# Centring a mixing matrix on TensorE, taking a variance by squares on ScalarE, and building the expert tables once

## The reference, cut to what matters

```
x = x + layernorm(attn(layernorm(x)))      # first half
x = x + layernorm(moe(layernorm(x)))       # second half

attn(y): Q, K, V = y Wq' + bq, y Wk' + bk, y Wv' + bv
         Q, K scaled to unit norm over the tokens
         tailor = 1 / (256 + Q . (sum K + 1e-6));  matrix = K' V
         return y + gamma * (sum V + Q matrix) * tailor
moe(y):  the two best of 8 experts for each token, e(y) = gelu(y W1 + b1) W2 + b2, plus a shared layer
layernorm(z) = (z - mean z) / sqrt(var z + 1e-5)
```

## Time and profile before

| | |
|---|---|
| time before, median of 3 runs | 691.05 us (690.42 to 691.43) |
| the profiled execution's own time | 688.41 us |
| its span | 686.6 us |
| PE busy | 590.0 us (86%), 4903 instructions |
| DVE busy | 465.6 us (68%), 1242 |
| ACT busy | 444.1 us (65%), 875 |
| POOL busy | 321.1 us (47%), 511 |
| mean granted TensorE clock | 0.96 |

### The profile page before, as it was taken

The page is one execution under the profiler, slowest core; times in us unless marked ns, Lnnn a source line. Parts: engine busy times, 40 slices in busy tenths (PEclk is TensorE's granted clock), DMA queues, the critical chain, the costliest instruction groups (busy, mean ns, idle before and its releaser), DMA issues.

```text
span 686.6 us, 16884 instructions
## 1 busy us (share of the span) xinstructions
PE 590.0 (86%) x4903; PEld 510.2 (74%) x4903; DVE 465.6 (68%) x1242; ACT 444.1 (65%) x875; POOL 321.1 (47%) x511
## 2 busy tenths in 40 slices
PE   4768988988887799999998999999999999999400
PEld 3657776777765588989897787989898998988300
DVE  5469999999987664544677676544444445778884
ACT  2647577677755584757555878757575665877653
POOL 4000234533626833578757332334343455664694
PEclk9989999999999999999999999999999999999855
DMA  7645564562155332113114221221211259641566
GB/s 250 213 149 188 184 185 125 185 220 86 66 170 202 105 128 79 48 34 95 33 47 126 79 63 49 75 82 48 79 56 48 56 106 226 118 94 61 115 163 122
DMA packets 45273, 78.25 MB, mean 114 GB/s; under 512 B 16963, under 2 KB 30597, under 8 KB 44805
## 3 DMA queue, kind: packets, MB, share of 16 engines
q1 hardware_dynamic: 33492, 48.19, 21.6%
q0 software_dynamic: 11696, 28.98, 17.6%
HBM read 48.17 MB, written 28.98 MB: 112 GB/s over the span
## 4 chain that ended last, share of the span: by engine, by line
PE 50%; DVE 29%; issue 8%; ACT 7%; POOL 3%; DVEq 1%; DMA 1%; ACTq 1%; POOLq 0%
PE banks L537 13%; PE banks L538 13%; PE banks L539 13%; ACT X L1531 3%; DVE st L1618 3%; PE banks L1209 2%; DVE W L1764 2%; DVE W L1768 2%; PE banks L1107 2%; ACT W L1391 1%; DVE zone L1707 1%; PE banks L1039 1%; DVE stage L1997 1%; PE banks L974 1%; ACT stage L1537 1%
## 5 line engine op out<-in xcount | busy, mean ns | idle before, releaser
L1531 ACT ACTIVATE X<-banks,b1T,tab 128x256 f32<-128x256 f32 x256 | 129.0, 553 | 101.2 <-PE banks L539 79.6
L1997 DVE SCALAR_TENSOR_TENSOR stage<-X,tab,stage 128x512 f16<-128x512 f32 (+1 forms) x160 | 109.3, 697 | 118.5 <-ACT stage L1537 112.7
L537 PE MATMUL banks<-W,stage 128*128 x576 | 157.1, 273 | 3.8 <-DVE stage L1997 2.4
L538 PE MATMUL banks<-W,stage 128*128 x576 | 157.0, 273 | 0.0
L539 PE MATMUL banks<-W,stage 128*128 x576 | 157.0, 273 | 0.0
L537 PE MATMUL banks<-X,W 128*128 128x256 f16 x512 | 140.3, 274 | 5.0 <-DVE X L2011 3.9
L538 PE MATMUL banks<-X,W 128*128 128x256 f16 x512 | 140.3, 274 | 0.0
L539 PE MATMUL banks<-X,W 128*128 128x256 f16 x512 | 140.2, 274 | 0.0
L839 POOL DMA_INDIRECT y_rows<-X,tb x72 | 81.4, 1131 | 102.4 <-DVE X L2028 77.8
L1537 ACT ACTIVATE stage<-X,tab 128x512 f16<-128x512 f32 (+1 forms) x160 | 106.9, 677 | 10.7 <-ACT X L1531 6.9
L826 POOL DMA_INDIRECT X<-xf_rows,tb x72 | 75.0, 1041 | 55.1 <-issue 34.2
(11 more groups left out here) (301 smaller groups left out, 1147.7 us busy)
## 6 DMA issues: line engine op xcount, KB each, us to landing
stage<-in_L_ffn_W SPq DMA_DIRECT2D x10, 1024.0 KB, 10.5
W<-in_L_ffn_W SPq DMA_DIRECT2D x6, 1024.0 KB, 7.3
X<-in_L_attn_x SPq DMA_DIRECT2D x8, 512.0 KB, 5.0
out<-X SPq DMA_DIRECT2D x8, 512.0 KB, 3.4
xf_rows<-zone SPq DMA_DIRECT2D x8, 512.0 KB, 4.1
u_rows<-b2b SPq DMA_DIRECT2D x8, 512.0 KB
X<-y_rows POOLq DMA_DIRECT2D x8, 512.0 KB, 8.1
away<-W SPq DMA_DIRECT2D x1, 2048.0 KB, 7.5
```

What stands on the lines that cost most here:

```text
L537: pe.matmul(o, lh, rh, start=first, stop=False)
L538: pe.matmul(o, lh, rl, start=False, stop=False)
L1531: a.activation(tile, tile if joint(j) else PS[m][:, r * BT:(r + 1) * BT], ACT.Gelu, bias=b1T[:, bass.ds(e * NH + 2 * m + r, 1)], scale=tab ...
L1997: v.scalar_tensor_tensor(o[1], src, tab[:, 1, bass.ds(e, 1)], o[0], ALU.mult, ALU.subtract).then_inc(h_low, 1)
```

## The change

Four things change.

1. The matrix that is transposed gets its unit and is centred by TensorE. `ident2` now holds I - 1/256 in place of I. `turn_mix` is no transpose any more: for each half f it multiplies the 128x128 identity by the half of `ident2` (this adds I - 1/256), and adds two products of the mixing matrix's blocks with `ident2`. The result, (M + I)(I - 1/256), has outputs whose mean is zero.
2. `mixT_out` is therefore a plain copy, and it is moved from VectorE to ScalarE: in a step behind `shared_out` 2, in the last step behind `mix_scale`, ahead of the two copies of the expert's weights.
3. Since the mean of z is zero, its variance is the mean of its squares. `attended` leaves VectorE. ScalarE takes four squares with a running sum (`z_square`), and the root from these sums (`z_spread`). `c2` is gone, and GpSimd's L903 becomes a multiplication by -1.
4. Of `expert_tables` only the bit mask stays in each step (`expert_powers`); three operations over all experts together (`all_tables`) run once, in the last step. `expert_bounds` has three operations for four. ScalarE's first gelu waits for the tables.

Beside these the scratch of GpSimd's DMA descriptors is set to 8192 bytes of a partition (it was not set before), and `z_dump` takes 4 KB of a partition.

```diff
-            g.memset(ident2, 0.0).then_inc(wide_set, 1)
+            g.memset(ident2, -1.0 / D).then_inc(wide_set, 1)
...
-            g.affine_select(out=ident2, in_=ident2, compare_op=ALU.not_equal, fill=1.0, base=0,
+            g.affine_select(out=ident2, in_=ident2, compare_op=ALU.not_equal, fill=1.0 - 1.0 / D, base=0,
...
-                g.tensor_tensor(shift_o[:, lo:hi], c2[:, lo:hi], shift_o[:, lo:hi], ALU.subtract).then_inc(last_shift, 1)
+                g.tensor_scalar(shift_o[:, lo:hi], shift_o[:, lo:hi], -1.0, None, ALU.mult).then_inc(last_shift, 1)
...
             def turn_mix(b):
                 pe.wait_ge(mix_scaled, NF * (b + 1))
                 pe.wait_ge(mixT_ready, b)
+                pe.wait_ge(wide_set, 2)
                 for f in range(NF):
+                    o = COS_PS[:, f * D:(f + 1) * D]
+                    pe.matmul(o, ident32, ident2[:, f, :], start=True, stop=False)
                     for n in range(NF):
-                        mm = pe.transpose(COS_PS[:, f * D + n * P:f * D + (n + 1) * P], ymix[:, n, f * P:(f + 1) * P], ident32)
+                        mm = pe.matmul(o, ymix[:, n, f * P:(f + 1) * P], ident2[:, n, :], start=False, stop=(n == NF - 1))
                 mm.then_inc(mix_turned, 1)
...
+            def mixT_out(b):                                   # ScalarE
+                a.wait_ge(mix_turned, b + 1)
+                a.wait_ge(z_ps, b)
+                settle(a)
+                a.activation(mixT, COS_PS.rearrange("p (f d) -> p f d", f=NF), ACT.Copy).then_inc(mixT_ready, 1)
+
+            def z_square(b):
+                a.wait_ge(z_ps, b + 1)
+                a.wait_ge(z_dev, b)
+                a.wait_ge(z_squares, T * b)
+                settle(a)
+                for t in range(T):
+                    a.activation(z_dump[:, t, :], Z_PS[:, t, :], ACT.Square, accum_out=z_sq[:, t:t + 1]).then_inc(z_squares, 1)
+
+            def z_spread(b):
+                a.wait_ge(z_squares, T * (b + 1))
+                a.wait_ge(z_factor, b)
+                settle(a)
+                a.activation(sd[:, 1, :], z_sq[:, :], ACT.Sqrt, bias=eps[:, 2:3], scale=1.0 / D).then_inc(z_dev, 1)
...
             def step(s):                                       # ScalarE
                 if i is not None:
                     w2_square(i)
+                if leaving is not None:
+                    z_square(leaving)
                 if mixing is not None:
                     xT_out(mixing, 1)
                     uk_out(mixing)
                 if leaving is not None:
-                    spread(1, z_dev, (z_mean, T * (leaving + 1)), 2, 1.0)
+                    z_spread(leaving)
...
                     shared_out(leaving, 2)
+                if mixing is not None:
+                    mixT_out(mixing)
                 if entering is not None:
                     xT_out(entering, 0)
...
             def last_step():                                   # ScalarE
-                spread(1, z_dev, (z_mean, T * b), 2, 1.0)
+                z_square(b - 1)
                 xT_out(b, 1)
                 uk_out(b)
+                z_spread(b - 1)
...
                 mix_scale(b)
+                mixT_out(b)
                 w1_highs(E - 1)
                 w2_highs(E - 1)
...
-            spread(1, z_dev, (z_mean, T * B), 2, 1.0)
+            z_square(B - 1)
+            z_spread(B - 1)
...
-            def mixT_out(b):                                   # VectorE
-                v.wait_ge(mix_turned, b + 1)
-                v.wait_ge(z_ps, b)
-                v.tensor_tensor(mixT, COS_PS.rearrange("p (f d) -> p f d", f=NF), ident2, ALU.add).then_inc(mixT_ready, 1)
-
-            def attended(b):
-                stats(1, b, lambda t: Z_PS[:, t, :], lambda t: [(z_ps, b + 1)], z_stats_t, z_mean)
...
-                v.scalar_tensor_tensor(c2[:, b * T:(b + 1) * T], mv[:, 1, :, 0], -1.0, cf[:, 1, :], ALU.mult, ALU.mult).then_inc(z_shift, 1)
...
+            def all_tables():
+                link = chain(v, expert_steps, EV * E)
+                link(v.tensor_scalar(einv[:, :, :].bitcast(I32), escl[:, :, :].bitcast(I32), -1.0, EXP_FLIP, ALU.mult, ALU.add))
+                link(v.tensor_scalar(gelu_scale[:, :], einv[:, 0, :], 1.0 / SX, None, ALU.mult))
+                link(v.tensor_tensor(down_scale[:, :], einv[:, 1, :], einv[:, 2, :], ALU.mult))
...
-    nc = _bacc.Bacc("TRN2", target_bir_lowering=False, num_devices=1)
+    nc = _bacc.Bacc("TRN2", target_bir_lowering=False, num_devices=1, dynamic_dma_scratch_size=8192)
```

More of the change, by code:

```diff
@@ L1404, in w1_highs @@
                 settle(a)
-                a.activation(w1_part(slot(i), 0), staged(i, 0), ACT.Copy, scale=escl[:, 0:1]).then_inc(w1_high, 1)
+                a.activation(w1_part(slot(i), 0), staged(i, 0), ACT.Copy, scale=escl[:, 0, TURN[i]:TURN[i] + 1]).then_inc(w1_high, 1)
             def w2_highs(i):
@@ L1410, in w2_highs @@
                 settle(a)
-                a.activation(w2_part(slot(i), 0), staged(i, 1), ACT.Copy, scale=escl[:, 1:2]).then_inc(w2_high, 1)
+                a.activation(w2_part(slot(i), 0), staged(i, 1), ACT.Copy, scale=escl[:, 1, TURN[i]:TURN[i] + 1]).then_inc(w2_high, 1)
             def step(s):
@@ L1537, in gelu @@
                         a.activation(hhl[:, j % 2, 2 * m:2 * m + 2, 0, span(j, p)], h32[:, m % 2, :].rearrange("p (r n) -> p r n", r=2)[:, :, span(j, p)],
-                                     ACT.Copy, scale=tab[:, 1, bass.ds(e, 1)]).then_inc(h_high, 1)
+                                     ACT.Copy, scale=high_scale[:, bass.ds(e, 1)]).then_inc(h_high, 1)
             def lean_of(j):
@@ L1886, in step @@
                     enter_factors(entering)
-                if leaving is not None:
-                    attended(leaving)
                 if entering is not None:
@@ L1918, in step @@
                     w1_lows(i)
-                if mixing is not None:
-                    mixT_out(mixing)
                 if s == B - 2:
@@ L1929, in last_step @@
                 b = B - 1
-                attended(b - 1)
                 products(b)
@@ L1943, in last_step @@
                 xf_low(b - 1)
-                mixT_out(b)
                 w1_lows(E - 1)
@@ L2086, in add_last @@
                     v.wait_ge(final_sum, lo + k + 1)
-            attended(B - 1)
             residual(B - 1)
```

56 lines of the change are left out of this document (28 added, 28 removed).

## The result

The changed kernel takes 701.67 us (median of 4 runs, 700.26 to 702.43), the kernel before took 691.21 beside it (4 runs, 690.42 to 691.43): ratio 1.0151, 95% interval 1.013 to 1.0172. It is slower, and 701.67 lies 0.8 us under the forecast of 702.5. The sum of the forecast was +11.5 us, the medians differ by 10.5. The two profiled executions differ by more, 14.1 us of span (700.7 and 686.6), since that of before lay 2.8 us under the median of its runs and that of after 0.8 over its own.

What follows compares the result with a forecast made beforehand. VectorE was taken to set the pace of the steps before, a chain through PE and ScalarE after. Five steps +6.2, the step before them +1.5, first step 0, last step +3.8: +11.5 on 691.05, 702.5 us; 8-in-10 range 697 to 707.

Steps and rivals of the forecast that it cites:

- The sum: Whole kernel: all stretches together +11.5 us, added to the median of 691.05 us, giving 702.5 us.
- The step: Five steps from 74.06 us: each 25.8 us against 24.56, together +6.2 us.
- The second step: Step from 50.05 us, 24.01 us before, without `count` on PE: 25.5 us, +1.5.
- VectorE's relief: In a step, 3.35 us of work taken off VectorE was to buy 1.0 us.
- The Trainium skill's factor of 4: `turn_mix`: FP32 transposes 4 times faster would make six matmuls 5.3 us; the forecast took 2.65 us from rows.
- The first step: Step from 22.86 us: taken as 0, between -1 (copy earlier) and +2.6 (lower clock).
- The last stretch: Last `weigh` to first expert block: +3.8 us together, between +2.2 (PE's share alone) and +5.5.
- all six at the lower level: First step's upper bound: all six `turn_mix` matmuls at 1.2 GHz, +2.6 us.
- +3.1 for `shared` 0: Last step: `shared` 0 starts at 221.9 instead of 218.90 us, behind `mixT_out`, ScalarE's weight copies and `xfT_out`.
- PE's waits: Rival, steps: PE's waits close, the step falls to 23.9 us, together -2.3, 688.8 us; chance 0.08.
- Squares at 0.58 us: Rival, ScalarE becomes the bound: squares 0.58 us in place of 0.37, +3.4, 706 us; chance 0.07.
- The scratch: Rival, last chain: GpSimd's DMAs wait for room in the smaller scratch, +8, 711 us; chance 0.05.

Runs made afterwards that it cites:

- unit early: Changed kernel with the unit's two matmuls as one of 512 columns, issued ahead of `shared` 0; 721.89 us, ratio 1.0055 to the kernel before.
- the filled variant: Changed kernel with PE kept at work by eleven unused f32 matmuls in its waits of the last step; 727.81 us, ratio 1.0141 to the kernel before.
- after, again: The changed kernel itself, unaltered, run once more on another chip; 730.01 us against 721.04 for the kernel before, ratio 1.0118.
- squares ahead: Changed kernel with the last sequence's `z_square` and `z_spread` ahead of the four `shared_out` of the last step; 728.07 us, ratio 1.0122 to the kernel before.
- copy behind: Changed kernel with `mixT_out` of the last step behind ScalarE's two weight copies; 725.8 us, ratio 1.0101 to the kernel before.
- unit on VectorE: Changed kernel with TensorE only centring, VectorE adding `ident2`, and ScalarE's matrix copy gone; 725.38 us, ratio 1.006 to the kernel before.
- and squares between: As unit on VectorE, with the last sequence's squares and root between the second and third shared copies; 728.3 us, ratio 1.0092 to the kernel before.

## Why the prediction was right, point by point

**The step.** Forecast 25.8, measured 25.56. The pieces held: `shared` 0 starts 16.42 after `weigh` (118.96) for 16.4, `turn_mix` 17.83 for 17.8, takes 2.61 for 2.65, `shared` 3 and half of `turn_x` 1.22 for 1.2 to 1.4; from `attend` to the next `weigh` it is 3.89 for 3.99. So +5.02 us over the five steps for +6.2, the excess being three pieces (the product, the one ahead of `attend`, the one behind it) that were each taken 0.1 too long. The second step is +1.40 for +1.5.

**What sets a step** is shown by three lengths of the same product. In the second step `turn_mix` is four transposes, four wide matmuls or six:

| `turn_mix` | its length | second step |
|---|---|---|
| transposes | 0.44 us | 23.24 us |
| four matmuls, unit early or on VectorE | 1.75 us | 24.55, 24.54 us |
| six matmuls | 2.62 us | 25.41 us |

1.31 us of step for 1.31 of product, then 0.86 for 0.87: one for one. VectorE's relief by contrast gave 0.77 us here and 1.13 in the third step, where the forecast put 0.7 and 1.0 on it.

**The Trainium skill's factor of 4** ("TensorE: Matmul & The Clock Gate", Terms) would have made the product 5.3 us. At the full clock it took 2.61, so the row's price holds. That 5.29 us stand in the last step is no support for it: there it is the clock, as the filled variant shows with 2.69.

**The first step.** Forecast 0, between -1 and +2.6; measured +0.96, and +0.56 ahead of the first `weigh`, for which I had nothing. `turn_mix` took 4.33 us (42.29 to 46.62) at a granted clock of 0.61, and `attend` starts 24.16 us after `weigh` in place of 21.24, +2.92. But `attend` then took 3.56 us at 1.00 where it had taken 5.52 at 0.64, and this paid two thirds back. Neither number is firmly the change's: in the five profiles whose first step has the changed kernel's list, that step takes 27.07 to 28.29 us, and the first `weigh` starts between 21.89 and 23.54.

**The last stretch: the term that was mis-sized.** Forecast +3.8 with a bound of +5.5, measured +6.45. From row to row: `turn_mix` starts 15.67 after `weigh` in place of 17.04, -1.37 (forecast -0.8; `mix` starts 0.77 sooner, as forecast, and the other 0.60 is `mix` itself, faster by the clock in this run); it takes 5.29 in place of 0.49, +4.80 (forecast +2.22); from its end to `shared` 0 it is 5.88 in place of 4.51, +1.37 (forecast +0.9 for the copy and the queue behind it); from there to the first block 8.63 in place of 6.98, +1.65 (forecast +1.5). The order of events was right and the price of one was taken at the full clock. The kernel before gave a reason for that, since its own `turn_mix` ran at 1.00 in this place, and a warning: the earlier trace rows gave this stretch a granted clock of 0.94 and the earlier trace rows an idle of 2.67 us right ahead of the product. For the first step I had set a bound with "all six at the lower level"; here I left it out. With it the bound would have been some 2.6 us higher. (By its own rows the forecast's +3.1 for `shared` 0 is +3.0.)

**The last stretch in nine profiles.** Cut in the same way, in us; the first column is counted from the last `weigh`:

| | `turn_mix` starts | its length | its end to `shared` 0 | `shared` 0 to first block | last stretch |
|---|---|---|---|---|---|
| before | 17.04 | 0.49 | 4.51 | 6.98 | 29.02 |
| after | 15.67 | 5.29 | 5.88 | 8.63 | 35.47 |
| after, again | 15.77 | 5.28 | 5.88 | 9.28 | 36.21 |
| unit early | 16.44 | 1.83 | 5.84 | 8.63 | 32.74 |
| squares ahead | 16.79 | 5.28 | 5.93 | 7.17 | 35.17 |
| PE kept at work | 15.73 | 2.69 | 5.84 | 9.32 | 33.58 |
| copy behind | 16.78 | 5.28 | 4.60 | 9.10 | 35.76 |
| unit on VectorE | 17.07 | 3.57 | 5.40 | 9.87 | 35.91 |
| and squares between | 17.08 | 3.57 | 5.51 | 10.59 | 36.75 |

The first column moves by 1.1 us among kernels whose lists are the same up to there (15.67, 15.77, 16.79, 16.78): that is `mix` at one or the other level of the clock, and no single stretch can be compared closer than that. In the fourth column 8.63 comes back with the unit early, and what others have above it can be read off ScalarE. It copies each of the four shared products out (`shared_out`); its other semaphores are met by the first copy, so the later ones wait for TensorE alone. In the changed kernel the last of these copies starts 0.42 us after the recorded start of its product's last matmul, in the repetition 1.07:

```profile
234.83 0.28 PE L1079 MATMUL banks<-b2b 128*128 128x264 f16 x1
235.25 0.48 ACT L1387 ACTIVATE b2b<-banks,der 128x264 f32<-128x264 f32 x1 [0.31 <-PE banks L1079]
```
```profile
241.85 0.28 PE L1079 MATMUL banks<-b2b 128*128 128x264 f16 x1
242.92 0.48 ACT L1387 ACTIVATE b2b<-banks,der 128x264 f32<-128x264 f32 x1 [0.95 <-PE banks L1079]
```

That is 0.65 us late, and the fourth column is 0.65 longer. With PE kept at work it is 0.70 late for 0.69 longer, with the copy behind 0.47 for 0.47, with the unit on VectorE 1.25 for 1.24, with the unit early 0 for 0. So in these executions TensorE delivered the last shared products later than its records say, and the first block was late by just that.

**The sum.** Against the two profiled executions (14.1) it is 2.6 too low: 1.3 too much for the steps, 2.7 too little for the last stretch, 1.5 too little for the first step and what lies ahead of it, 0.3 too much for the blocks. Against the medians (10.5) it is 1.0 too high, which is why the predicted time came within 0.8 us. Part of that closeness is luck, since the two profiled executions lie on opposite sides of their medians, and these runs don't tell which stretches make the 3.6 us between the two differences.

**The rivals.** PE's waits did not close: 0.72 us at L1086, 1.25 at `shared` 0 and 0.24 within it stand in a step of after. Squares at 0.58 us: 0.36 to 0.37. The scratch: no effect.

## What stays open

On the three other chips every kernel here lost 20 to 30 us more. Part lies in the steps from the third on, where GpSimd writes the slots, and where the granted clock of some steps is 0.94 to 1.00; most lies in the expert blocks: in the kernel with only the scratch changed PE is busy 404.9 of the first 423.1 us at a granted clock of 0.97, with 3687 matmuls recorded, where the first chip has 410.3 at 1.00 with 3854. In the two variants with early squares VectorE's copy of the first block's tokens then starts 2.0 and 5.9 us past the recorded end of the transposes that feed it, with no releaser in the profile. TensorE ran later there than its records say, since ScalarE's last shared copy came 0.9 and 1.9 us late in the sense of the table above; why it did, and what the rest of the 2.0 and 5.9 us is, is open. In spite of it the squares ahead of the shared copies gave the shortest way from `shared` 0 to the first block of all versions of the changed kernel, 7.17 us against 8.63 or more, in one execution, and the squares between gave the longest, 10.59. Whether either pays on the whole kernel is not shown, and they were not run on the first chip. Nor is it shown what decides where the clock falls in the last step.

## What to carry to other kernels

Before work is moved off the busiest engine, follow the chain of the other engines through one period without it: that is the most the move can win (here 0.8 to 1.1 us a step for 3.35 us of work), and whatever the move puts on that chain costs its full length (here 2.17 us for 2.18). If such work is unavoidable, put the part that needs no late input into a wait of the same engine: the unit's 0.88 us became free in that way. Price a TensorE product behind an idle of some us at the lower clock as well as at the full one, since behind the same 2.67 us it was 1.00 in one kernel here and 0.50 in the other. And cut a stretch into its pieces before you call a variant useless: the piece that was changed can have gained what another lost.

## What was not expected of the hardware

- The same six f32 matmuls took 2.61 us at a granted clock of 1.00 and 5.29 at 0.50, behind an idle of 2.67 us; with eleven unused matmuls in front of them, 2.69. Matmuls that compute nothing of use gave back 2.6 us of the product, and 1.9 to 2.6 of its stretch.
- With one and the same list of work up to its end, `mix` took 2.68, 2.74, 3.79 and 3.79 us in the last step of four profiles.
- What another engine sees of TensorE can be later than TensorE's own records: by 0 to 1.9 us at the last shared product.
- f32 transposes cost half of an f32 matmul's time for a column (four of 128 columns 0.43 us, one of 256 columns 0.441).
- A ScalarE square with a running sum, 128x256 out of PSUM, costs 0.36 to 0.37 us in a row, since its READ_ACCUMULATOR of 0.2 us runs beside the next.
- Chips differ: the same kernel took 691 us on one, 717 and 721 on others, and by stretch the difference ranged from nothing (the second step, 24.01 or 24.02 us where the product was not changed, 25.40 or 25.41 where it was) to 6% (from the first block to the end, 460.7 and 487.3).
